# Output biases from rows weighted by GpSimd and summed by TensorE, in two attention layers

## The chip, the cores and the metric

The kernel runs on one core of a Trainium2 chip. Its time is that of the device in microseconds, the median of 3 runs. Beside it there is one execution taken by the hardware profiler, whose span runs from the first to the last instruction.

## The reference

Two layers in a row, each a group normalisation, a self-attention over 1024 positions of 256 channels, an output projection with a bias, and a residual. Batch 2, all in float32.

```python
xn = group_norm(x, gamma, beta)                      # 32 groups of 8 channels
q, k, v = xn @ wq + bq, xn @ wk + bk, xn @ wv + bv   # 1024 x 256 each
attn = softmax(q @ k.T / 16)                         # 1024 x 1024
out = (attn @ v) @ wp + bp + x
```

Because each row of `attn` sums to one, the bias of `v` contributes the same row `bv @ wp` to every output row. The kernel adds `bv @ wp + bp` once per output row. That vector of 256 numbers per layer is the output bias of the title.

## The kernel before

**Algebra.** The scores are computed as `xn @ A @ xn.T` with `A = wq @ wk.T`, and the values as `xn @ Wx` with `Wx = wv @ wp`, so that a unit (one image in one layer, four units in all) needs three kinds of large product: `t` (`A` times the normalised input), the scores `S`, and the values `V`, and then the attention product `O`. Each large product is made of three matmuls with rounded operands (`_hi` and `_lo` parts, whose sum is the float32 value): `L1081` to `L1083` for t, `L1108` to `L1110` for scores, `L1094` to `L1096` for values, `L1134` to `L1136` for attention.

**Order.** All engines run programs written out by hand, in the order of the code, with semaphores between them. There is no scheduler. PSUM holds seven banks used in a ring (`ring`) and one more, `X`. Bank 6 of the ring (`RING - 1`) serves the small things of the start: the warm-up products, group means and variances, and the output bias. Its later use by the third score tile waits for `dv_ob`, which says that the output bias was taken out.

**The start.** SyncE issues all loads in one queue: `wq`, `wk` of layer 0, image 0, `wv`, `wp`, then `wq`, `wk` of layer 1, `wide` of layer 0 (rows of the vectors copied to all 128 partitions), `wv`, `wp` of layer 1, `wide` of layer 1, then `moved` (image 1, in pieces of 128 bytes for the transposition by VectorE) and image 1 itself. Layers, units and images are counted from 0, as in the code. In the rows the numbers of buffers are left out, so `w_wp` is either layer's.

**TensorE's start** (in this order): transposes of the weights (`transpose_weight`, L939), of image 0 (L985), the product A of layer 0 (L948), one-column products of layer 0's `wp` with `bv` (L970), group means (L1021) and group variances (L1027), Wx of layer 0 (L957), the one-column products of layer 1, A of layer 1, the first half of Wx of layer 1, the first half of t, the second half of Wx, the second half of t, four transposes that spread the bias columns over all partitions (L978), and then the scores of the first half (chunk 0).

**The statistics.** VectorE sums up group statistics (`channel_statistics`, L637), TensorE averages over groups, VectorE adds epsilon (L653), GpSimd raises to the power -0.5 (`power`, L348), and VectorE makes gain and shift and normalises (L678). ScalarE rounds to `xn_hi` (L457), VectorE subtracts to `xn_lo` (L685). The t products read both.

**What follows on VectorE.** `t_lo` (L714), `A_lo` of layer 1, `out_bias` (L631), `Wx_lo` of layer 1 (L613), then image 1's transposes and statistics between the running maxima of chunk 0 (L732), the values' low parts (L721), and the query maxima and their shift (`neg_shift`, L746), which TensorE spreads over the partitions in `shift_to_all` (L1127). GpSimd adds the output bias to the image rows (`residual`, L359) and forms the low parts of the exponentials (`p_low`, L363).

## Time and profile before

| what | value |
|---|---|
| median of 3 runs | 253.14 us (253.07 to 253.24) |
| span of the profiled execution | 250.6 us |
| the profiled execution's own time beside its span | not given by the page |
| TensorE busy | 245.2 us, 98% of the span |
| VectorE busy | 187.2 us, 75% |
| ScalarE busy | 149.4 us, 60% |
| GpSimd busy | 125.1 us, 50% |
| mean granted TensorE clock | 0.999 |

The span is 2.5 us shorter than the median time, because it leaves out what lies before the first and behind the last instruction. A share of busy time is an average over the whole span, so it does not say which engine is waited for in a given stretch. The views used below are the chain of waits, which follows the work that ended last backwards from the last instruction, and timelines of single engines.

### The profile page before, as it was taken

How to read it: one execution, taken by the hardware profiler on the slowest of the kernel's cores; microseconds unless marked ns; L12 is line 12 of the kernel's file. 1: busy time of each engine (PE TensorE's matmuls, PEld its weight loads, DVE VectorE, ACT ScalarE, POOL GpSimd, SP SyncE). 2: the span in 40 equal slices, each digit the busy share in tenths (PEclk: the TensorE clock that was granted, in tenths of full speed). 3: DMA queues.
4: the chain of work that ended last, by engine and by line, in shares of the span. 5: the costliest groups of instructions: out<-in, count | busy, mean ns of one | idle time of the engine just before them, and what ended most of it. 6: DMA issues, size and time to landing. Idle time of an engine off the chain costs nothing.

```text
span 250.6 us, 4585 instructions
## 1 busy us (share of the span) xinstructions
PE 245.2 (98%) x1570; PEld 223.5 (89%) x1570; DVE 187.2 (75%) x490; ACT 149.4 (60%) x291; POOL 125.1 (50%) x151
## 2 busy tenths in 40 slices
PE   7999998999999999999999999999999999999995
PEld 6888888889998899889998899889998899889995
DVE  0688898888994798587975998587875798449804
ACT  3665543699994309831998508940998509740920
POOL 3010621485779306901797916901797918800870
PEclk9999999999999999999999999999999999999999
DMA  6999000000025002320142001320110000100112
GB/s 195 352 153 221 6 0 3 0 1 3 0 86 86 1 0 55 84 32 3 43 87 43 0 0 46 84 41 3 43 43 0 3 16 29 42 0 10 36 42 86
DMA packets 34767, 12.37 MB, mean 49 GB/s; under 512 B 26284, under 2 KB 34488, under 8 KB 34744
## 3 DMA queue, kind: packets, MB, share of 16 engines
q1 hardware_dynamic: 34720, 12.07, 20.0%
q8 instruction: 13, 0.21, 0.4%
q14 instruction: 10, 0.08, 0.1%
q10 hardware_dynamic: 24, 0.01, 0.0%
HBM read 7.88 MB, written 4.19 MB: 48 GB/s over the span
## 4 chain that ended last, share of the span: by engine, by line
PE 89%; DVE 6%; DMA 2%; issue 1%; ACT 1%; SPq 0%; DVEq 0%
PE ring L1134 12%; PE ring L1136 12%; PE ring L1135 12%; PE ring L1109 10%; PE ring L1110 10%; PE ring L1108 10%; PE ring L1081 3%; PE ring L1083 3%; PE ring L1082 3%; PE ring L1094 3%; PE ring L1096 3%; PE ring L1095 2%; DVE R L732 2%; DMA xnat<-in_x 2%; PE ring L948 1%; DVE xraw L593 1%
## 5 line engine op out<-in xcount | busy, mean ns | idle before, releaser
L363 POOL TENSOR_TENSOR P_lo<-S,P_hi 128x512 fp32r<-128x512 f32 x64 | 81.9, 1310 | 52.2 <-ACT S L503 52.1
L1134 PE MATMUL ring<-V,P_hi 128*128 128x258 f32 x256 | 72.7, 284 | 0.0
L1136 PE MATMUL ring<-V,P_lo 128*128 128x258 f32 x256 | 72.4, 283 | 0.0
L1135 PE MATMUL ring<-V,P_hi 128*128 128x256 f32 x256 | 72.3, 282 | 0.0
L502 ACT ACTIVATE P_hi<-S 128x512 fp32r<-128x512 f32 x64 | 40.4, 631 | 29.7 <-DVE S L791 29.7
L495 ACT COPY S<-ring 128x512 f32<-128x512 f32 x64 | 36.6, 590 | 31.4 <-PE ring L1110 30.3
L1108 PE MATMUL ring<-t_hi,xn_lo 128*128 128x512 f32 x128 | 49.9, 390 | 0.0
L1109 PE MATMUL ring<-t_lo,xn_hi 128*128 128x512 f32 x128 | 49.8, 389 | 0.0
L1110 PE MATMUL ring<-t_hi,xn_hi 128*128 128x512 f32 x128 | 49.8, 389 | 0.0
L1134 PEld LDWEIGHTS ring<-V,P_hi 128*128 128x128 f32 x256 | 48.5, 189 | 0.4
L1135 PEld LDWEIGHTS ring<-V,P_hi 128*128 128x128 f32 x256 | 48.4, 189 | 0.4
L1136 PEld LDWEIGHTS ring<-V,P_lo 128*128 128x128 f32 x256 | 48.5, 190 | 0.0
L732 DVE TENSOR_TENSOR R<-ring,R 128x512 f32<-128x512 f32 x48 | 32.9, 685 | 12.5 <-ACT S L495 10.9
L791 DVE TENSOR_TENSOR S<-X,S 128x512 f32<-128x512 f32 x64 | 41.1, 681 | 0.0
L503 ACT ACTIVATE S<-S 128x512 f32<-128x512 f32 x64 | 40.0, 625 | 0.0
L359 POOL TENSOR_TENSOR xnat<-xnat,out_bias 128x256 f32<-128x256 f32 x32 | 22.5, 746 | 13.4 <-DVE out_bias L631 13.4
L1110 PEld LDWEIGHTS ring<-t_hi,xn_hi 128*128 128x128 f32 x128 | 24.0, 188 | 5.0
L1108 PEld LDWEIGHTS ring<-t_hi,xn_lo 128*128 128x128 f32 x128 | 24.0, 188 | 4.7
L1109 PEld LDWEIGHTS ring<-t_lo,xn_hi 128*128 128x128 f32 x128 | 24.0, 188 | 4.7
L348 POOL TENSOR_TENSOR r<-var_e,minus_half 128x2 f32<-128x2 f32 x4 | 2.8, 709 | 37.3 <-DVE var_e L653 37.3
L721 DVE TENSOR_TENSOR V<-ring,V 128x256 fp32r<-128x256 f32 x32 | 13.4, 418 | 8.9 <-ACT V L488 8.9
L1094 PE MATMUL ring<-Wx_hi,xn_lo 128*128 128x258 f32 x64 | 18.6, 290 | 0.0
(117 smaller groups left out, 356.3 us busy)
## 6 DMA issues: line engine op xcount, KB each, us to landing
xnat<-in_x SPq DMA_DIRECT2D x8, 256.0 KB, 4.6
between<-xnat SPq DMA_DIRECT2D x16, 128.0 KB, 1.8
out<-xnat SPq DMA_DIRECT2D x16, 128.0 KB, 1.7
moved<-in_x SPq DMA_DIRECT2D x8, 128.0 KB, 4.7
moved<-between SPq DMA_DIRECT2D x16, 64.0 KB, 2.4
moved<-between SPq DMA_DIRECT2D x32, 32.0 KB, 2.0
w_wq<-in_L_conv_wq SPq DMA_DIRECT2D x2, 256.0 KB, 4.3
w_wk<-in_L_conv_wk SPq DMA_DIRECT2D x2, 256.0 KB, 4.5
```

Source lines behind the costliest of these rows:

```text
L363: nc.gpsimd.tensor_tensor(P_lo[:, exp_of(c, kb), :], S[:, tile_of(c, kb), :], P_hi[:, exp_of(c, kb), :].bitcast(F32), ALU.subtract).then_i ...
L495: nc.scalar.copy(S[:, tile_of(c, kb), :], bank_of("S", c, kb)[:]).then_inc(ac_S, 1)
L502: nc.scalar.activation(P_hi[:, exp_of(c, kb), :], S[:, tile, :], ACT.Exp)
L503: nc.scalar.activation(S[:, tile, :], S[:, tile, :], ACT.Exp).then_inc(ac_P, 1)
L732: nc.vector.tensor_tensor(R[:], bank_of("S", c, kb)[:], earlier, ALU.max).then_inc(dv_R, 1)
L791: nc.vector.tensor_tensor(tile, X[:], tile, ALU.add).then_inc(dv_D, 1)
L1108: nc.tensor.matmul(bank[:], xn_lo[:, kc, keys], t_hi[:, kc, cols], start=(kc == 0), stop=False)
L1109: nc.tensor.matmul(bank[:], xn_hi[:, kc, keys], t_lo[:, kc, cols], start=False, stop=False)
L1110: last = nc.tensor.matmul(bank[:], xn_hi[:, kc, keys], t_hi[:, kc, cols], start=False, stop=(kc == KC - 1))
L1134: nc.tensor.matmul(bank[:, 0:C + 2], P_hi[:, tile, mine], v[:, kb, 0:C + 2], start=(kb == 0), stop=False)
L1135: nc.tensor.matmul(bank[:, 0:C], P_hi[:, tile, mine], v[:, kb, C + 2:VX], start=False, stop=False)
L1136: last = nc.tensor.matmul(bank[:, 0:C + 2], P_lo[:, tile, mine], v[:, kb, 0:C + 2], start=False, stop=(kb == NB - 1))
```

## The change

The output bias of a layer is `bv @ wp + bp`. Before, TensorE multiplied blocks of `wp` with the column `bv` (8 products of one column in all), VectorE added `bp` as a column (`bias_columns`), TensorE transposed the broadcast columns so that every partition held the row, and VectorE copied the result out of PSUM. After, GpSimd multiplies the rows of `wp` by `bv` per partition, adds the two blocks and splits the sum into a rounded and a remaining part (`weighted_rows`). TensorE multiplies both parts with a 128x128 matrix of ones, which sums over the partitions and leaves the row in each of them. VectorE adds `bp`, which now comes with `wide`, as it takes the result out of PSUM. The second half of layer 1's Wx product moves from the middle of the t products to behind the first half.

```diff
-WIDE = VECTORS[3:5]
+WIDE = VECTORS[3:6]
...
-        bias_col = sb("bias_col", [P, LAYERS, KC])
+        ones = sb("ones", [P, P], F32R)
...
+            weighted = sb("weighted", [P, LAYERS, KC, C], stack=early)
+            weighted_hi = sb("weighted_hi", [P, LAYERS, C], F32R, stack=early)
+            weighted_lo = sb("weighted_lo", [P, LAYERS, C], F32R, stack=early)
...
+            def weighted_rows(l):
+
+                r = l * NV + VECTORS.index("bv")
+                pool.wait_ge(ld_w[l, "wp"], 16)
+                for k in range(KC):
+                    nc.gpsimd.tensor_scalar(weighted[:, l, k, :], w_raw[l, "wp"][:, k, :], vec_cols[:, k, r:r + 1],
+                                            None, ALU.mult).then_inc(po_bv, 1)
+                pool.wait_ge(po_bv, 5 * l + 2)
+                nc.gpsimd.tensor_tensor(weighted[:, l, 0, :], weighted[:, l, 0, :], weighted[:, l, 1, :], ALU.add
+                                        ).then_inc(po_bv, 1)
+                pool.wait_ge(po_bv, 5 * l + 3)
+                nc.gpsimd.tensor_copy(weighted_hi[:, l, :], weighted[:, l, 0, :]).then_inc(po_bv, 1)
+                pool.wait_ge(po_bv, 5 * l + 4)
+                nc.gpsimd.tensor_tensor(weighted_lo[:, l, :], weighted[:, l, 0, :], weighted_hi[:, l, :].bitcast(F32),
+                                        ALU.subtract).then_inc(po_bv, 1)
...
+            weighted_rows(0)
             power(0)
+            weighted_rows(1)
             pool.wait_ge(dv_ob, 1)
...
+            nc.vector.memset(ones[:].bitcast(F32), 1.0)
...
-            def bias_columns():
-                dve.wait_ge(pe_ob, LAYERS)
-                for l in range(LAYERS):
-                    nc.vector.tensor_tensor(bias_col[:, l, :], bias_bank(l), vec_cols[:, :, l * NV + VECTORS.index("bp")],
-                                            ALU.add).then_inc(dv_oc, 1)
-
             def output_biases():
                 dve.wait_ge(pe_oa, 1)
-                nc.vector.tensor_copy(out_bias[:, :, :], ring[RING - 1][:, :].rearrange("p (l c) -> p l c", l=LAYERS)
-                                      ).then_inc(dv_ob, 1)
+                for l in range(LAYERS):
+                    dve.wait_ge(ld_wide[l], 16)
+                    last = nc.vector.tensor_tensor(out_bias[:, l, :], ring[RING - 1][:, l * C:(l + 1) * C],
+                                                   wide[:, l, WIDE.index("bp"), :], ALU.add)
+                last.then_inc(dv_ob, 1)
...
-            def output_bias(l):
-
-                pe.wait_ge(ld_w[l, "wp"], 16)
-                if l:
-
-                    pe.wait_ge(dv_stat, VARE)
-                r = l * NV + VECTORS.index("bv")
-                for k in range(KC):
-                    for kd in range(KC):
-                        last = nc.tensor.matmul(bias_bank(l)[:, k:k + 1], w_raw[l, "wp"][:, kd, k * P:(k + 1) * P],
-                                                vec_cols[:, kd, r:r + 1], start=(kd == 0), stop=(kd == KC - 1))
-                last.then_inc(pe_ob, 1)
-
             def output_biases_to_all():
-                pe.wait_ge(dv_oc, LAYERS)
-                for l in range(LAYERS):
-                    for k in range(KC):
-                        last = nc.tensor.transpose(ring[RING - 1][:, l * C + k * P:l * C + (k + 1) * P],
-                                                   bias_col[:, l, k:k + 1].to_broadcast([P, P]), ident[:])
-                last.then_inc(pe_oa, 1)
+
+                pe.wait_ge(po_bv, 5 * LAYERS)
+                nc.tensor.matmul(ring[RING - 1][:], ones[:], weighted_hi[:, :, :].rearrange("p l c -> p (l c)"),
+                                 start=True, stop=False)
+                nc.tensor.matmul(ring[RING - 1][:], ones[:], weighted_lo[:, :, :].rearrange("p l c -> p (l c)"),
+                                 start=False, stop=True).then_inc(pe_oa, 1)
...
-            output_bias(0)
             mean_of_groups(0)
...
-            output_bias(1)
             for mc in range(KC):
                 A_product(1, mc)
-            Wx_product(1, 0)
+            for mc in range(KC):
+                Wx_product(1, mc)
...
-            Wx_product(1, 1)
```

On TensorE, from layer 0's transposed `wv` to the first t product, the program before reads:

```order
L939 MATMUL X<-ident,w_wv 128x128 x4
L970 MATMUL ring<-vec_cols,w_wp 128x1 x4
L1021 MATMUL ring<-mv,group_mean 128x2
L939 MATMUL ring<-ident,w_wq 128x128 x4
L939 MATMUL ring<-ident,w_wk 128x128 x4
L1027 MATMUL ring<-var_c,group_mean 128x2
L957 MATMUL ring<-w_wp,wvT 128x256 x4
L939 MATMUL X<-ident,w_wv 128x128 x4
L970 MATMUL ring<-vec_cols,w_wp 128x1 x4
L948 MATMUL ring<-wkT_bk,wqT 128x257 x4
L957 MATMUL X<-w_wp,wvT 128x256 x2
L1081 MATMUL ring<-xn_hi,A_lo 128x512
```

and of the changed program the same place reads as follows (its lines are those of the changed file: L953 transposes weights, L962 is A, L971 is Wx):

```order
L953 MATMUL X<-ident,w_wv 128x128 x4
L1022 MATMUL ring<-mv,group_mean 128x2
L953 MATMUL ring<-ident,w_wq 128x128 x4
L953 MATMUL ring<-ident,w_wk 128x128 x4
L1028 MATMUL ring<-var_c,group_mean 128x2
L971 MATMUL ring<-w_wp,wvT 128x256 x4
L953 MATMUL X<-ident,w_wv 128x128 x4
L962 MATMUL ring<-wkT_bk,wqT 128x257 x4
L971 MATMUL X<-w_wp,wvT 128x256 x4
L1081 MATMUL ring<-xn_hi,A_lo 128x512
```

Both groups of four one-column products are gone, and the Wx product of layer 1 is there in full (x4 where x2 stood) ahead of t.

On GpSimd, from the copies of `bk` into the weights to layer 0's first residual, the program before has three rows:

```order
L393 COPY wkT_bk<-vec_cols 128x2 x2
L348 TENSOR_TENSOR r<-var_e,minus_half 128x2
L359 TENSOR_TENSOR xnat<-xnat,out_bias 128x256 x8
```

and the changed one has:

```order
L408 COPY wkT_bk<-vec_cols 128x2 x2
L354 TENSOR_SCALAR weighted<-w_wp,vec_cols 128x256 x2
L357 TENSOR_TENSOR weighted<-weighted 128x256
L360 CAST weighted_hi<-weighted 128x256
L362 TENSOR_TENSOR weighted_lo<-weighted,weighted_hi 128x256
L347 TENSOR_TENSOR r<-var_e,minus_half 128x2
L354 TENSOR_SCALAR weighted<-w_wp,vec_cols 128x256 x2
L357 TENSOR_TENSOR weighted<-weighted 128x256
L360 CAST weighted_hi<-weighted 128x256
L362 TENSOR_TENSOR weighted_lo<-weighted,weighted_hi 128x256
```

Five rows of layer 0 now stand ahead of the power (L348, now L347), five of layer 1 behind it.

## Rows read from the trace of the kernel before

**Rows 1.** The page, part 1: busy time, share of the span, instructions.
```profile
PE 245.2 (98%) x1570; PEld 223.5 (89%) x1570; DVE 187.2 (75%) x490; ACT 149.4 (60%) x291; POOL 125.1 (50%) x151
```

**Rows 2.** TensorE's waits: who waited for whom, us in total, times, longest.
```profile
...
PE X L1127 <- DVE neg_shift L746: 0.7, 1, 0.7
...
```

**Rows 3.** The chain of waits, 8 to 43 us: start, us, what.
```profile
...
10.51 0.79 PE ring L970 x8
11.30 0.23 PE ring L1021 x2
...
14.90 0.79 PE ring L970 x8
...
17.53 0.86 PE X L957 x4
...
21.20 0.86 PE X L957 x4
...
24.63 0.25 PE ring L1083
24.91 0.70 ACT t_hi L481
...
26.38 0.60 DVE out_bias L631
26.98 0.66 DVE Wx_lo L613 x2
...
42.09 0.65 PE X L1127 x4
...
```

**Rows 4.** Timeline of VectorE: start us, us, instruction, count.
```profile
10.65 0.39 DVE L637 BATCH_NORM_AGGREGATE mv<-bn 128x2 f32<-128x24 f32 x2
...
16.16 1.28 DVE L685 TENSOR_TENSOR xn_lo<-xraw,xn_hi 128x512 fp32r<-128x512 f32 x2
...
19.43 1.28 DVE L685 TENSOR_TENSOR xn_lo<-xraw,xn_hi 128x512 fp32r<-128x512 f32 x2
```

**Rows 5.** Timeline of TensorE's products: first and middle of t, the four transposes.
```profile
18.04 0.58 PE L1081 MATMUL ring<-xn_hi,A_lo 128*128 128x512 f32 x1
...
21.71 0.58 PE L1081 MATMUL ring<-xn_hi,A_lo 128*128 128x512 f32 x1
...
24.70 0.60 PE L978 MATMUL ring<-ident,bias_col 128*128 128x128 f32 x4
...
25.06 0.48 PE L1108 MATMUL ring<-t_hi,xn_lo 128*128 128x512 f32 x1
```

**Rows 6.** DMA: layer 0's `wp`, `moved`; each with its landing times.
```profile
4.34 0.47 SPq L282 DMA_DIRECT2D w_wp<-in_L_conv_wp  x1
...
DMA to landing us min/median/max: 5.5/6.2/6.8
...
L305 SPq DMA_DIRECT2D moved<-in_x x8: 432/875/3763, 8.3 to 18.6; - x8
...
DMA to landing us min/median/max: 4.0/4.7/8.0
```

**Rows 7.** GpSimd: timeline rows, and the summary of L363 (ns min/median/max).
```profile
12.97 0.72 POOL L348 TENSOR_TENSOR r<-var_e,minus_half 128x2 f32<-128x2 f32 x1 [7.41 <-DVE var_e L653]
27.05 5.63 POOL L359 TENSOR_TENSOR xnat<-xnat,out_bias 128x256 f32<-128x256 f32 x8 [13.36 <-DVE out_bias L631]
...
63.34 1.70 POOL L363 TENSOR_TENSOR P_lo<-S,P_hi 128x512 fp32r<-128x512 f32 x1 [2.96 <-ACT S L503]
...
L363 POOL TENSOR_TENSOR P_lo<-S,P_hi x64: 1280/1302/1695, 48.8 to 241.5; 128x512 fp32r<-128x512 f32 x64
```

**Rows 8.** Stretches: length, busy us by engine, granted clock, DMA share, GB/s.
```profile
3.70:5.80 2.10, 1.69 (x12) 1.24 (x11) 0.18 (x1) 0.96 (x2) 0.31 (x2) 1.00 0.91 264
5.80:9.00 3.20, 2.86 (x20) 2.44 (x21) 1.29 (x4) 1.96 (x5) 0.00 (x0) 1.00 1.03 351
```

**Rows 9.** VectorE's L685, all eight (ns min/median/max).
```profile
L685 DVE TENSOR_TENSOR xn_lo<-xraw,xn_hi x8: 678/682/684, 16.2 to 65.6; 128x512 fp32r<-128x512 f32 x8
```

More of the change, by code:

```diff
@@ L188, in two_attention_layers @@
         po_bk = sem("po_bk")
+        po_bv = sem("po_bv")
         po_resid = sem("po_resid")
@@ L198, in two_attention_layers @@
         pe_Wx = sem("pe_Wx")
-        pe_ob = sem("pe_ob")
         pe_oa = sem("pe_oa")
@@ L226, in two_attention_layers @@
         dv_Wx = sem("dv_Wx")
-        dv_oc = sem("dv_oc")
         dv_ob = sem("dv_ob")
@@ L244, in two_attention_layers @@
         dv_O = sem("dv_O")
-        def bias_bank(l):
-            return ring[RING - 1][:, (l + 1) * KC:(l + 2) * KC]
         def mean_bank(v):
@@ L705, in _ @@
             normalise(0, range(2, 4))
-            bias_columns()
             Wx_low(0, 1)
```

## The prediction

> **What bounds the kernel now.** I read the page's engine shares first: TensorE is busy for 98% of the span [rows 1]. So the question is where TensorE still stands still, and whether an edit touches that place or TensorE's own queue. The list of TensorE's waits has one entry behind the ninth microsecond: 0.7 us in which the transposes of `shift_to_all` (L1127) wait for VectorE's `neg_shift` [rows 2]. Behind it TensorE runs to the tail without a wait that the list shows, so what moves that point moves the end.
>
> The chain of waits shows what leads up to it [rows 3]. From 8.6 to 24.9 us it is TensorE in its own order: weights, the two groups of one-column products (L970), the products A and Wx, the t products. At 24.91 it passes over `t_hi` on ScalarE to `t_lo`, `out_bias` and `Wx_lo` on VectorE, stays on VectorE for image 1's statistics and the running maxima, and comes back to TensorE at 42.09. So there are two stretches to price: TensorE before 24.9 us, and VectorE from 25.6 to 42.0 us. Between them TensorE is not the bound: it has 0.7 us to spare at 42.09.
>
> **The change part by part.**
>
> *The one-column products.* Two groups of 8 (4 products, each shown as two passes) take 0.79 us each in the chain [rows 3]. The second group, at 14.90, stands between transposes and `A_product(1, 0)`, which wait for nothing there: removing it gives 0.79. The first, at 10.51, stands ahead of the group means (L1021), which need the aggregate that VectorE finishes at 10.65 + 0.39 = 11.04 [rows 4]; the means begin at 11.30. So at most 0.26 is to be had. A part goes to the handover and to the empty array: four transposes behind the wait at 42.09 take 0.65 [rows 3], four in a full queue 25.06 - 24.70 = 0.36 [rows 5]. That difference, 0.29, would eat all of it. The bounds are 0 and 0.2; I take 0.05, near the lower one, as the row after a wait is the same situation.
>
> A rule would price the group otherwise. The row gives 0.79 / 8 = 0.10 us per one-column pass. The Trainium skill's page "TensorE: Matmul & The Clock Gate", section "Wait — 56ns, not 53.3ns?", says that starts of small matmuls lie no closer than about 25 ns: by that alone a group would be worth 0.2 us and the sum would shrink to a gain of about 0.2. The trace disagrees with that as a price for these products; the same page's section on LDWEIGHTS (columns / 1.2 GHz, 107 ns for 128) comes near the row, so it is the weights that are paid for.
>
> *Wx of layer 1* (the second of two, as the code counts). Its second half (L957, 0.86 us at 21.20) moves ahead of the t products, behind the first half at 17.53 [rows 3]. The start of the t products goes 0.86 later, their end doesn't move. So t starts at 18.04 - 0.79 - 0.05 + 0.86 = 18.06, as before; its second half, which began at 21.71 [rows 5], begins 0.84 earlier, at 20.87, and its last product, which ended at 24.63 + 0.25 = 24.88, ends 0.84 earlier too. Are the operands there? `xn_lo` for the first half is done from 16.16 + 0.64 = 16.80 on, for the second from 19.43 + 0.64 = 20.07 on [rows 4]. The tighter slack is 20.87 - 20.07 = 0.80. The two small additions `bias_col` that leave VectorE between them can only widen it.
>
> *GpSimd's rows.* Per layer two products by a scalar, an addition, a rounding and a subtraction, each 128x256. Layer 0's five stand ahead of `power(0)`, on which the normalisation, `xn_lo` and the t products hang. They start when `wp` of layer 0 has landed: 4.34 + 5.5 = 9.84 [rows 6]. `power(0)` started at 12.97 [rows 7] and may slip by the slack of 0.80, to 13.77: the five may take 3.9 us. The nearest rows: 8 two-input additions of this shape take 5.63, 0.70 each; the P_lo subtraction that also writes rounded output takes 1.30 for twice the elements, 0.65 [rows 7]. As an upper bound all five at 0.70, with 0.06 for each of four handovers (an estimate, twice the 0.03 us between the last t product's end and `t_hi`): 3.75. As a lower one, the three with one input at half: 2.6. I take 3.2, so they end near 13.0, delay `power(0)` by nothing or 0.1, and cost nothing. If that cover is gone, each further microsecond comes out as one of delay. Layer 1's five follow `power(0)` and are needed only by the product at 24 us; with GpSimd idle until 27.05 [rows 7] they are hidden.
>
> [...]
>
> *The sum with ones.* Four transposes (0.36) give way to two products of 512 columns. A 512-column product in the stream takes 0.25 in the chain [rows 3], so 0.5: TensorE loses some 0.14, behind the last t product. The 0.7 us of its wait at 42.09 cover it.
>
> *VectorE.* `out_bias` was one copy of 512 columns, 0.60 in the chain; it becomes two additions of 256 out of PSUM. Two such subtractions (`Wx_lo`) take 0.66 [rows 3]: +0.06 on the path. Bounds: 0, and 0.23 if a start of their own adds half of one such addition, 0.17. `bias_col` was off the path here; the memset of `ones` falls in the idle first microseconds.
>
> *DMA.* `wide` grows from 2 to 3 KB in each of 128 partitions, 256 to 384 KB, twice. At the 351 GB/s of the early stretch [rows 8] that is 0.37 us for what is queued behind the first and 0.75 behind both. `moved` is behind both; the last of its eight issues starts at 18.6, and its first reader on VectorE starts behind `Wx_lo`, at 26.98 + 0.66 = 27.64 (26.86 after) [rows 3, 6]. With the median of 4.7 us to landing it is there at 23.3, and with 0.75 more still in time.
>
> *Sum*: -0.79 - 0.05 + 0.06 = -0.78 us on the path to `neg_shift`, and from there TensorE carries it to the end. The profiled execution has a span of 250.6 us, the timed runs a median of 253.14; the 2.5 us between lie around the span and don't change. 253.14 - 0.78 = 252.36. With the bounds: 252.1 (-0.79 - 0.2) to 252.6 (-0.79 + 0.23).
>
> **The rivals.**
> 1. *Partly absorbed, within 0.2%.* The gain must pass VectorE's chain of 16 us, where score copies, `moved` and the running maxima each have a few tenths to spare. For it: `moved` took up to 8.0 us to land at worst [rows 6]; were that the last issue (from about 18.6), it would land at 26.6 + 0.75 = 27.35 against 26.86, 0.49 late. Or the five rows take 4.3 instead of 3.2 and `power(0)` is 0.4 too late. Against it: of the eight issues one alone took 3763 ns where the median took 875, and the longest landing is more likely that one's than the last one's. Time: 253.14 - 0.78 + 0.45 = 252.8. Chance 0.20.
> 2. *GpSimd becomes the gate: slower.* One mechanism, the five rows ahead of `power(0)`. Nothing in the trace shows a 128x256 product by a per-partition scalar on GpSimd. If the two cost 1.6 each (more than twice the addition), the five take 5.5, end at 15.3, and t starts 1.6 late: 253.14 - 0.78 + 1.6 = 253.9. It decides from 3.9 + 0.78 = 4.7 us on. Against it: the two-input addition of this size takes 0.70, and here there is one input. Chance 0.06.
> 3. *The port.* GpSimd and VectorE disturb each other while both run. The row: P_lo at 63.34 took 1.70 against a median of 1.30 while VectorE ran two `xn_lo` subtractions, but these took 678 to 684 ns in all eight cases, GpSimd idle or not [rows 7, 9]. So GpSimd pays 0.2 per such neighbour and VectorE nothing; layer 0's rows meet only statistics and 2-column operations, layer 1's meet `xn_lo` and have time. If VectorE paid the same 0.4 for two `xn_lo` operations that the slack doesn't hold, twice: 253.14 - 0.78 + 0.8 = 253.2. Chance 0.03. The Trainium skill's "GPSIMD Engine Reference", section 8 ("Key points"), states the contention without a price or a loser.
> 4. *The clock.* TensorE will stand idle for about 0.6 us before the group means. It was idle for 0.4 of 2.1 us at 3.7 to 5.8 at a granted clock of 1.00, 2.4 GHz [rows 8]. A fall to 1.2 GHz that doubles 1 us of work costs 1 us: 253.4. Chance 0.02.
> 5. *The products were cheap.* The chain gives a busy stretch to whoever is in it; if only a quarter of the 0.79 is the passes' own and the rest is the start of what follows, the removal returns 0.2: 253.14 - 0.2 - 0.05 + 0.06 = 252.95. Against it: the half of Wx behind A and the half between the t products take the same 0.86 [rows 3], whatever stands ahead. Chance 0.03. The Trainium skill's rule on the spacing of small matmuls ("TensorE: Matmul & The Clock Gate", section "Wait — 56ns, not 53.3ns?") would have it so.
>
> **How the numbers follow.** The forecast has 0.66. A measurement of this kernel can tell some 0.2%, 0.5 us, from no change. Faster by more: the forecast and a little of rival 1, 0.69. Within: most of rival 1, and rivals 3 to 5 for the most part, 0.24. Slower: rival 2 and half of rival 4, 0.07. In the order of rivals: 0.66, then 0.20, 0.06, 0.03, 0.02, 0.03. The range from 252.0 to 253.0 holds the forecast with its bounds, rival 1 and rival 5, and leaves out rivals 2 to 4, 0.11; alone the forecast would span 252.1 to 252.6.
>
> **What would show it.** In the new trace: the group means 0 to 0.2 earlier; L1127's wait ending near 41.3; `t_hi` last starting near 24.1; `power(0)` starting by 13.1, at most 13.8; the two `out_bias` additions 0.66 together; TensorE's wait before L1127 0.5 to 0.7. Wrong it is if the t products wait for `xn_lo` (GpSimd's rows too long), or if TensorE's 42.09 stays while 24.91 moves (something on VectorE's stretch waits).

## The result: slower by 0.45%, where 0.3% faster was forecast

| | before | after |
|---|---|---|
| median | 253.08 us (253.01 to 253.24, 6 runs) | 254.05 us (253.74 to 255.48, 6 runs) |
| ratio to before, 95% interval | | 1.0045 (1.0031 to 1.0059) |
| profiled execution: own time, span | span 250.6 | 254.13, span 252.4 |

The forecast was 252.36 us, its range 252.0 to 253.0; the measured time lies outside. Two different things cost the time. I read them in the order in which they stand in the span: the stretch to the transposes of `shift_to_all` (L1127), and what is behind it.

**The page.** First part, busy time of each engine, and the instructions:

```profile
span 252.4 us, 4559 instructions
...
PE 245.4 (97%) x1552; PEld 222.0 (88%) x1552; DVE 188.6 (75%) x490; ACT 149.1 (59%) x291; POOL 133.2 (53%) x161
```

A pass is one matmul row of the trace; each of the 8 one-column products shows as two passes, a transpose and a product with rounded operands as one. TensorE has 18 passes fewer than in [rows 1] (16 of one column and 4 transposes gone, 2 products of 512 new) and nearly the same busy time (245.4 us for 245.2); VectorE has the same 490 instructions and is busy 1.4 us longer.

**The waits.** The list by engine and line: us in total, times, longest:

```profile
PE ring L1022 <- DVE mv L652: 0.9, 2, 0.7
...
PE ring L1081 <- DVE xn_lo L700: 0.8, 2, 0.5
...
PE X L1127 <- DVE neg_shift L760: 0.6, 1, 0.6
DVE xraw L611 <- DMA moved<-between: 0.6, 1, 0.6
```

The second is the sign that the prediction had named for "GpSimd's rows too long": both halves of t wait for `xn_lo`. The last has no counterpart before at all.

**GpSimd's timeline**, 8 to 30 us (start, us, engine, line, operation, tiles, count, idle before):

```profile
10.71 1.84 POOL L354 TENSOR_SCALAR weighted<-w_wp,vec_cols 128x256 f32<-128x256 f32 x2 [4.74 <-DMA w_wp<-in_L_conv_wp]
12.63 0.73 POOL L357 TENSOR_TENSOR weighted<-weighted 128x256 f32<-128x256 f32 x1
13.44 0.40 POOL L360 CAST weighted_hi<-weighted 128x256 fp32r<-128x256 f32 x1
13.91 0.73 POOL L362 TENSOR_TENSOR weighted_lo<-weighted,weighted_hi 128x256 fp32r<-128x256 f32 x1
14.60 0.73 POOL L347 TENSOR_TENSOR r<-var_e,minus_half 128x2 f32<-128x2 f32 x1
15.31 1.84 POOL L354 TENSOR_SCALAR weighted<-w_wp,vec_cols 128x256 f32<-128x256 f32 x2
17.23 0.78 POOL L357 TENSOR_TENSOR weighted<-weighted 128x256 f32<-128x256 f32 x1
...
18.63 1.18 POOL L362 TENSOR_TENSOR weighted_lo<-weighted,weighted_hi 128x256 fp32r<-128x256 f32 x1
```

Layer 0's five occupy GpSimd from 10.71 to 14.64, 3.93 us. The product by a per-partition scalar takes 0.92, more than the addition of two tiles (0.73); of the three operations with one input only the rounding (0.40) is as cheap as I had made all three.

**VectorE's timeline**, 11 to 21 us:

```profile
11.12 0.39 DVE L652 BATCH_NORM_AGGREGATE mv<-bn 128x2 f32<-128x24 f32 x2
...
13.14 0.22 DVE L668 TENSOR_SCALAR var_e<-ring,eps 128x2 f32<-128x2 f32 x1
...
15.36 0.16 DVE L675 TENSOR_TENSOR r0sq<-r 128x2 f32<-128x2 f32 x1 [1.61 <-POOL r L347]
...
16.75 1.54 DVE L693 TENSOR_SCALAR xraw<-xraw,gain,shift 128x512 f32<-128x512 f32 x2
...
18.55 1.81 DVE L700 TENSOR_TENSOR xn_lo<-xraw,xn_hi 128x512 fp32r<-128x512 f32 x2
...
20.98 0.99 DVE L693 TENSOR_SCALAR xraw<-xraw,gain,shift 128x512 f32<-128x512 f32 x2
...
22.23 1.28 DVE L700 TENSOR_TENSOR xn_lo<-xraw,xn_hi 128x512 fp32r<-128x512 f32 x2
```

The same operations in the kernel before:

```profile
13.72 0.16 DVE L660 TENSOR_TENSOR r0sq<-r 128x2 f32<-128x2 f32 x1 [0.45 <-POOL r L348]
...
14.90 1.00 DVE L678 TENSOR_SCALAR xraw<-xraw,gain,shift 128x512 f32<-128x512 f32 x2
```

`var_e` is done at 13.36, the power starts at 14.60. And the pairs at 16.75 and 18.55, which run while layer 1's five rows are on GpSimd, take 1.54 and 1.81; the same pairs behind them take 0.99 and 1.28, as in the kernel before (1.00 above, 1.28 in [rows 4]). From the start of `r0sq` to the end of the first `xn_lo` pair it is 5.00 us where it was 3.72. Of the `xn_lo` pair itself only the second operation is slow. The query for that tile, 18 to 21 us (ns min/median/max):

```profile
L700 DVE TENSOR_TENSOR xn_lo<-xraw,xn_hi x2: 675/944/1214, 18.6 to 19.2; 128x512 fp32r<-128x512 f32 x2
```

The one that began at 18.55, ahead of GpSimd's subtraction at 18.63, took its usual 0.68; the one that began at 19.15, inside that subtraction, took 1.21.

**The chain of waits**, 4 to 44 us:

```profile
4.76 5.85 DMA w_wp<-in_L_conv_wp
...
10.71 1.85 POOL weighted L354 x2
...
14.64 0.69 POOL r L347
...
23.05 0.47 PE ring L1081
...
26.10 0.70 ACT t_hi L498
...
27.49 0.75 DVE out_bias L645 x2
...
43.35 0.65 PE X L1127 x4
```

It begins with the landing of `wp` (4.76 + 5.85 = 10.61, where I had 9.84), goes over GpSimd's rows, the power and VectorE, and only then enters TensorE. L1127 starts at 43.35, 1.26 us later than in [rows 3]. Behind it the last matmul comes 205.86 us later, where it was 205.32 before: 0.54 more, at the wait for `moved<-between`.

**A yardstick.** The start is not the same in every execution of one kernel: the aggregate of image 0 (`BATCH_NORM_AGGREGATE` on VectorE) starts at 10.65 in the profile of before, and at 11.33 and 13.15 in two more profiles of the same kernel (below). So I compare two distances: A, from that aggregate to the transposes of `shift_to_all`, and B, from there to the start of the last matmul. Before: A 31.44, B 205.32. After: A 32.23, B 205.86. Together +1.33; the medians say +0.97. The rest would lie in the start, which the profiles don't settle: the aggregate of the changed kernel is at 11.12, later than in one profile of before and earlier than in two.

### The profile page after: what moved, and what is told of

It is laid out like the page before. It is cut to its first block, busy times and chain, and to the rows that moved or that the text cites. A ratio compares the mean times of both kernels' runs of the same rounds, so it can differ in the third digit from the quotient of the medians.

```text
span 252.4 us, 4559 instructions
## 1 busy us (share of the span) xinstructions
PE 245.4 (97%) x1552; PEld 222.0 (88%) x1552; DVE 188.6 (75%) x490; ACT 149.1 (59%) x291; POOL 133.2 (53%) x161
## 4 chain that ended last, share of the span: by engine, by line
PE 60%; DVE 20%; DMA 5%; SPq 4%; issue 4%; ACT 3%; POOL 2%; DVEq 0%; ACTq 0%
PE ring L1134 9%; PE ring L1136 9%; PE ring L1135 9%; PE ring L1108 7%; PE ring L1109 7%; PE ring L1110 7%; DVE R L746 3%; DVE S L805 3%; SPq L304 3%; DMA w_wp<-in_L_conv_wp 2%; DMA between<-xnat 2%; PE ring L1081 2%; DVE xraw L611 2%; PE ring L1082 2%; PE ring L1083 2%
## 5 line engine op out<-in xcount | busy, mean ns | idle before, releaser
L347 POOL TENSOR_TENSOR r<-var_e,minus_half 128x2 f32<-128x2 f32 x4 | 2.9, 714 | 30.4 <-DVE var_e L668 30.4
```

## The experiments

The first four experiments ask what GpSimd's rows cost, and in which way: the power comes late (theory 1), or VectorE is slower beside GpSimd (theory 2).

### e1_no_rows, e2_rows0_only, e3_rows1_only, e4_power_first

```diff
+            no_rows(0)
+            no_rows(1)
             pool.wait_ge(dv_const, 1)
...
-            weighted_rows(0)
             power(0)
-            weighted_rows(1)
```

This is e1: `no_rows` is two memsets of zero for a layer, in the idle start. e2 keeps `weighted_rows(0)`, with memsets for layer 1 behind the power; e3 keeps `weighted_rows(1)`, with memsets for layer 0 at the start. Memsets in place of rows leave bv @ wp out of the output of that layer. e4 is complete: `power(0)` stands ahead of both `weighted_rows`.

> The changed kernel without GpSimd's weighted rows: both parts are set to zero in the idle start, so the output lacks bv @ wp in both layers. Everything else, TensorE's order, the sum with ones, the wider load and VectorE's two additions, stays. Theory (only the rows on GpSimd were mis-priced; TensorE's and VectorE's terms of the prediction hold): the power starts as soon as its variance is there, within 0.1 us, t waits for nothing, and the time is 0.6 to 0.9 us under before, 252.2 to 252.5. Rival (the removal of the column products returns little, or the wider load delays the start by the 0.4 us seen in the changed kernel's profile): 252.8 or more.

> The changed kernel with layer 0's rows alone; layer 1's are set to zero behind the power, so layer 1's output lacks bv @ wp. Theory, two causes that add up: the rows ahead of the power delay it by some 1.2 us (they take 3.9 us from the landing of wp on), and the rows behind it slow VectorE's normalisation and xn_lo by some 1.3 us through the shared access to SBUF; t can hide 0.8 of the sum. So this run shows the first cause alone: power delayed by about 1.2, VectorE's first normalisation back at 0.54 us each, and a time about 0.4 us over the run without rows, near 252.7. Rival, the delay ahead of the power is all there is: the time is that of the changed kernel, 254.0.

> The changed kernel with layer 1's rows alone, behind the power; layer 0's are set to zero in the idle start, so layer 0's output lacks bv @ wp. Theory of the two causes: the power is on time, but VectorE between r0sq and the second xn_lo takes 4.9 us instead of 3.6, as in the changed kernel, and with 0.8 of slack the time is about 0.5 us over the run without rows, near 252.8. Rival, the delay ahead of the power is all there is: VectorE's stretch takes 3.6 us again and the time is that of the run without rows.

> All of the change, but the power stands ahead of both layers' rows, which then run one after the other, some 7.9 us, beside VectorE's normalisation and both pairs of xn_lo. Rival theory, only the delay of the power costs: 252.3 to 252.5, all of the predicted gain. Theory of the two causes: the power is on time, but VectorE loses 1.3 us before the first half of t and up to 1.0 more before the second; less 0.8 of slack that is 1 to 1.5 us over the run without rows, 253.3 to 253.9, so little is won against the changed kernel's 254.05.

| | median (runs), beside before 252.96 (31 runs) | ratio, 95% | A | B |
|---|---|---|---|---|
| e1, no rows | 253.15 (12) | 1.0002 (0.9986 to 1.0018) | 30.57 | 206.25 |
| e2, layer 0's | 253.27 (12) | 1.0016 (0.9994 to 1.0039) | 30.58 | 206.09 |
| e3, layer 1's | 253.48 (12) | 1.0020 (1.0003 to 1.0037) | 30.89 | 206.58 |
| e4, power first | 254.42 (8) | 1.0062 (1.0031 to 1.0093) | 31.83 | 206.21 |

e1's A is 0.87 below that of before, a little more than the forecast's whole sum, and 1.66 below that of the changed kernel: that is what the rows cost. e4 takes the power's delay away (`r0sq` starts 3.06 behind the aggregate, as the 3.07 of before) and is still slow. VectorE's timeline of e4 shows by what way:

```profile
14.36 0.16 DVE L675 TENSOR_TENSOR r0sq<-r 128x2 f32<-128x2 f32 x1 [0.43 <-POOL r L347]
...
15.78 1.55 DVE L693 TENSOR_SCALAR xraw<-xraw,gain,shift 128x512 f32<-128x512 f32 x2
...
17.59 1.81 DVE L700 TENSOR_TENSOR xn_lo<-xraw,xn_hi 128x512 fp32r<-128x512 f32 x2
```

So both theories hold, each with a part. e3, with layer 1's rows alone, lies between: its `xn_lo` pair takes 1.68, from `r0sq` to its end it is 4.29 where 4.9 was expected, and its A is 0.32 above e1's. e2 could not price the delay: the execution that was profiled started late (aggregate at 13.59), while `wp` landed at 10.74, and the five rows were done at 14.74, before the power was wanted (15.82). Its VectorE runs at its old pace (1.00 and 1.28), which fits theory 2, since layer 0's rows stand beside nothing large.

But e1 was expected to give back the forecast's gain and doesn't. Its B is 0.93 above that of before. All four have a wait for `moved<-between` of 0.7 to 1.3 us, near 170 us. So there is a second cause.

### b1_before, b2_before, e5_shifted, e6_no_columns

Is the late wait a matter of the execution, of where tiles lie, or of TensorE's program? b1 and b2 are the kernel before, unchanged. e5 is the kernel before with 480 unused bytes per partition, meant to put the tiles behind them where the changed kernel has them; the tiles of the start that lie behind the wider `wide` are not moved with it. e6 is the kernel before without the 16 one-column passes (`bias_col` is then bp alone, so bv @ wp is left out):

```diff
-            output_bias(0)
...
-            output_bias(1)
```

> The kernel before, unchanged, for a second profile. In all five profiles of changed kernels the aggregate of the group statistics came 0.4 us or more later than in the one profile of before, the first four transposes took 1.07 us where they took 0.76, and VectorE later waited 0.6 to 1.3 us for image 1's pieces of layer 1. Theory (that one execution was a fortunate one, and the start varies from run to run whatever the kernel): here the aggregate comes at 11.0 to 11.4 too, and the late wait is there. Rival (something in the change makes the start slower): all three are as in the first profile.

> The same once more, a third profile of the kernel before, with the same two readings.

> The kernel before with one unused tensor of 480 bytes per partition put in behind the bias columns, so that everything behind it lies where it lies in the changed kernel. Theory (the place in SBUF is nothing): no change in time and the same profile as before. Rival (the place is what slows the start): 0.3 to 0.7 us slower, first transposes 1.07 us, wait for the pieces of layer 1.

> The kernel before without the 16 one-column passes of TensorE: the bias columns hold bp alone, so the output lacks bv @ wp. Nothing else is changed: transposes, copy, load and the place of Wx stay. It prices the one term of the prediction that carries it. Theory (0.79 + 0.05 off TensorE's path, all of it passed on): 0.7 to 0.9 us faster than before. Rival (the start or VectorE's stretch swallows it, as the changed kernel without rows, which came out the same as before within 0.16%, suggests): within 0.3 us of before.

| | median (runs), beside before 253.09 (23 runs) | ratio, 95% | aggregate | A | B | late wait |
|---|---|---|---|---|---|---|
| b1 | 254.88 (1) | | 13.15 | 31.43 | 205.29 | none |
| b2 | 253.06 (1) | | 11.33 | 31.44 | 205.28 | none |
| e5 | 253.14 (12) | 0.9999 (0.9976 to 1.0021) | 10.77 | 31.39 | 205.38 | none |
| e6 | 252.43 (12) | 0.9972 (0.9955 to 0.9989) | 11.02 | 30.53 | 206.18 | 1.0 |

The places of the tiles moved by e5 do nothing. The late wait comes when passes are taken from TensorE, with or without GpSimd's rows. e6's A is 30.53 and e1's 30.57, so moving `Wx`, the two products with ones and the second addition of `output_biases` together cost 0.04.

The DMA view says where. Stretches of 3 us in 40 slices; `between<-xnat` is one of two writes that follow each other by 3.05 us, and on queue 8 one transfer of 0.02 MB appears (the slice with 218 GB/s when it stands alone). Before, 150 to 153 us:

```profile
GB/s 0 0 0 0 0 0 0 0 0 0 0 0 0 0 0 0 14 218 369 328 369 287 151 14 0 0 0 0 0 0 218 0 0 0 0 0 0 0 0 0
...
q8 instruction: 1, 0.02, 1.8%
...
between<-xnat SPq DMA_DIRECT2D x1, 128.0 KB, 1.7
```

The changed kernel, 155 to 158 us:

```profile
GB/s 0 0 0 0 0 0 0 0 0 382 273 355 328 300 192 28 0 0 0 0 0 0 0 0 0 14 14 0 14 14 0 14 14 14 14 0 0 0 0 0
...
q8 instruction: 1, 0.02, 2.6%
...
between<-xnat SPq DMA_DIRECT2D x1, 128.0 KB, 3.3
```

Before, the transfer of queue 8 stands 1.0 us behind the start of the first write, in the gap ahead of the second. In the changed kernel it begins in the same slice as the second write, and that write ends with a thin tail of 14 GB/s over 0.75 us that begins 0.7 us behind the burst: it lands after 3.3 us instead of 1.7. SyncE waits for it before it issues the eight reads `moved<-between` of 32 KB, and the chain of the changed kernel then goes through `154.85 3.27 DMA between<-xnat` to unit 3's statistics and the group means.

### e7_second_group_out, e8_padded, e9_after_padded, e10_rows_by_tensor

Queue 8 is marked "instruction". If it brings TensorE's program at fixed places of it, fewer passes ahead of that place let it come later against the work (theory F); the rival is that any earlier TensorE meets the writes worse (theory G). e7 removes one group alone:

```diff
-            output_bias(1)
```

e8 and e9 fill TensorE's program up again with products of one column that nothing reads. e8 is e7 with 6 of them in the warm-up in place of 2 of its 6 products of 128 columns; e9 is the changed kernel with this edit:

```diff
-            keep_running(6)
+            keep_running(3)
+            one_column(8)
...
+            one_column(4)
             mean_of_groups(0)
```

e10 is a complete kernel of a third kind: the row of bv @ wp comes ready and in all partitions out of TensorE, with bv's column broadcast as the stationary operand; bp is added from wide rows as in the changed kernel. It also has filler in the warm-up, 10 one-column products in place of 4 of the 6 of 128 columns.

```diff
-                        last = nc.tensor.matmul(bias_bank(l)[:, k:k + 1], w_raw[l, "wp"][:, kd, k * P:(k + 1) * P],
-                                                vec_cols[:, kd, r:r + 1], start=(kd == 0), stop=(kd == KC - 1))
+                    last = nc.tensor.matmul(ring[RING - 1][:, l * C:(l + 1) * C],
+                                            vec_cols[:, kd, r:r + 1].to_broadcast([P, P]),
+                                            w_raw[l, "wp"][:, kd, :], start=(kd == 0), stop=(kd == KC - 1))
```

> The kernel before without the second group of one-column products (16 passes become 8); the first group stays, its result is not read, the bias columns hold bp alone, so the output lacks bv @ wp. Open is where the late wait of unit 3's statistics comes from (VectorE waits 0.6 to 1.3 us for moved<-between near 167 us in the six kernels whose TensorE has 16 passes fewer, in none of the four that have them). Theory F: TensorE's own instructions are fetched by DMA (13 transfers on queue 8), at fixed places of its program; with 16 passes fewer the fetch that began 0.95 us behind the start of the first of two writes to `between` begins 2.9 us behind it, together with the second write, which then takes 3.3 us instead of 1.8. With 8 fewer it should begin about 1.9 behind, between the two: no late wait, shift_to_all 30.65 us behind the aggregate (31.44 before, less 0.79), 252.3 us. Theory G: any earlier TensorE meets the writes worse, and the place in the program is nothing: a late wait of 0.6 to 1.3 here too, and 252.6.

> The kernel before without both groups' use: the first group stays as an unread filler in its own place, the second is gone from the path, and the warm-up at the start holds 8 one-column passes more than before (4 products of 128 columns and 6 of one column, where there were 6 of 128), so TensorE's program has as many passes as before; the output lacks bv @ wp. Theory F: the fetch stands 0.95 us behind the first write's start as before, no late wait, shift_to_all 30.65 us behind the aggregate, 252.3 us as in the kernel with 8 fewer. Theory G: late wait 0.6 to 1.3, 252.6 or more. If one-column passes at the start let the granted clock fall, or end later than 4.05 us, it is slower by what the start then shows.

> The changed kernel with 18 one-column passes of no use: 8 in TensorE's wait ahead of the group means, the others in the warm-up at the start (3 products of 128 columns and 8 of one, for 6 of 128), so that everything behind stands at the place in TensorE's program that it had before the change. Theory F: the fetch is back between the two writes, the late wait of 0.6 us on VectorE is gone, and the time falls from 254.05 by 0.5 to 0.6 (last matmul minus shift_to_all 205.3 instead of 205.86): 253.5. Theory G: 254.05 and the wait stays. The rows of GpSimd and VectorE's slower operations beside them stay in either case: shift_to_all 32.2 us behind the aggregate.

> A complete version meant to beat both: no work on GpSimd. TensorE multiplies bv's column, broadcast as the stationary operand, with wp (two products of 256 columns per layer, 1.03 us for four passes of 257 in A's rows); layer 0 in the wait of 0.7 us ahead of the group means, layer 1 in place of the four transposes behind t; bp is added out of wide rows as in the changed kernel, Wx stays in its old order, and 12 one-column passes pad the start. Expected from the rows: -0.79 -0.05 for the groups, +0.33 for layer 0's 1.03 in a wait of 0.7, +0.06 for the two additions, +0 to 0.1 for layer 1's 1.03 in place of 0.36 against 0.66 of slack: -0.45 to -0.35, 252.7. Theory F: no late wait. Theory G: with it 253.2. If the wait ahead of the means is only the 0.26 of the profiled execution before, 0.4 more.

| | median (runs), beside before 253.06 (17 runs) | ratio, 95% | aggregate | A | B | late wait |
|---|---|---|---|---|---|---|
| e7 | 252.19 (12) | 0.9981 (0.9956 to 1.0006) | 13.01 | 30.54 | 205.25 | none |
| e8 | 254.48 (6) | 1.0063 (1.0045 to 1.0081) | 13.41 | 30.54 | 205.30 | none |
| e9 | 255.64 (4) | 1.0105 (1.0092 to 1.0119) | 14.35 | 31.06 | 205.40 | none |
| e10 | 255.67 (4) | 1.0107 (1.0092 to 1.0121) | 15.08 | 30.74 | 205.37 | none |

The times of e8 to e10 miss what I expected of them (252.3, 253.5 and 252.7): in the start, where most of the filler stands, a one-column pass takes 0.21 us (e8: 12 of them in 2.42 us), and the aggregate starts 2 to 4 us later than in b2. B doesn't depend on that, and it speaks for F: in all four it is back at 205.3 to 205.4 and the wait is gone. G is out, since e7's TensorE is 0.9 us earlier and meets no late wait. The count of passes says the same. From the span's start to the start of queue 8's transfer, before and in the changed kernel (in the order of the columns: length, then PE, PEld, DVE, ACT, POOL, each with its instructions, granted clock, DMA share, GB/s):

```profile
0.00:152.25 152.25, 149.74 (x927) 134.98 (x928) 120.58 (x329) 92.76 (x184) 71.70 (x98) 1.00 0.26 61
```

```profile
0.00:155.68 155.68, 151.80 (x927) 135.50 (x928) 123.40 (x332) 94.53 (x188) 81.65 (x110) 1.00 0.24 61
```

In both, TensorE has begun 927 passes by then. The changed kernel has 18 fewer in its start, so its 927th stands later in the work. In all sixteen traces of this case it is 925 to 931.

e7's median (252.19, expected 252.3) has executions with early and late starts in it, from 251.44 to 254.70, so its interval is wide. Its trace tells what each group is worth. One group out gives 31.44 - 30.54 = 0.90, both give 0.91: the second group is worth 0.90 and the first 0.01.

e9 gives the price of the two ways of GpSimd as well, by the accident of its late start: `wp` had landed, the rows began at 9.83 and the power waited for `var_e`, not for them. Between e1 and e9 it is 31.06 - 30.57 = 0.49, VectorE's slowing alone behind the slack; from the changed kernel to e9 it is 32.23 - 31.06 = 1.17, as much as the power's delay (`r0sq` 4.24 us behind the aggregate there, 3.07 in e9). One trace each stands behind this split.

### e11_rows_by_tensor_unpadded, e12_after_gap_filled

e11 is e10 without the filler. e12 is the changed kernel with 8 one-column passes in TensorE's wait ahead of the group means and nothing else:

```diff
+            one_column(4)
             mean_of_groups(0)
```

> The complete version with bv's column as the stationary operand, without the filler in the start, where a one-column pass took 0.21 us and made the whole run start 2 to 3 us late. TensorE has 12 passes fewer than the kernel before, so by theory F the fetch begins about 2.4 us behind the first write's start, just ahead of the second at 2.9: no late wait, shift_to_all 30.74 us behind the aggregate as with the filler (31.44 before), 252.4 us. Rival: 12 fewer is already too many, the fetch meets the second write, a late wait of 0.6 to 1.3 and 252.9 to 253.2.

> The changed kernel with 8 one-column passes of no use in TensorE's wait of 0.9 us ahead of the group means (0.12 us each there), nothing changed in the start; 10 passes fewer than before instead of 18. Theory F: the fetch stands about 2.2 us behind the first write's start, between the writes: no late wait, the last matmul 205.3 us behind shift_to_all instead of 205.86, 253.5 us against 254.05. Theory G (an earlier or later phase of the writes, not the place in the program): wait and time stay, 254.05. shift_to_all 32.2 us behind the aggregate as in the changed kernel; in the version whose start was late by the filler it was 31.06, because wp had landed by then: if the landing of wp decides, a late start here too gives less than 32.2.

| | median (runs), beside before 253.10 (18 runs) | ratio, 95% | A | B | late wait |
|---|---|---|---|---|---|
| e11 | 252.50 (252.00 to 252.71, 8) | 0.9973 (0.9963 to 0.9983) | 30.75 | 205.39 | none |
| e12 | 253.42 (253.06 to 254.58, 11) | 1.0020 (1.0008 to 1.0032) | 32.08 | 205.40 | none |

Both came out within 0.1 us of what F gave (252.4 and 253.5). e12 has more work than the changed kernel and its ratio is 0.0025 lower, 0.6 us, with intervals that touch only at their ends (1.0008 to 1.0032, and 1.0031 to 1.0059). Of the 0.6, 0.46 is in B (205.40 for 205.86) and 0.15 in A. Its DMA view, 155 to 158 us:

```profile
GB/s 218 0 0 0 0 0 0 0 0 0 0 0 68 205 369 341 341 260 110 14 14 27 0 0 0 0 0 0 0 0 0 0 0 0 0 0 0 0 0 0
...
q8 instruction: 1, 0.02, 2.0%
...
between<-xnat SPq DMA_DIRECT2D x1, 128.0 KB, 2.0
```

The transfer of queue 8 is ahead of the second write by 0.9 us, and the tail is short. Over the kernels, the place of that transfer behind the start of the first write, the passes that TensorE has fewer than before, and the landing of the second write:

| passes fewer | 0 (before, b1, b2, e5, e9) | 8 (e7) | 10 (e12) | 12 (e11) | 16 (e6) | 18 (after; e1 to e4) |
|---|---|---|---|---|---|---|
| behind the first write's start, us | 1.0 | 1.8 | 2.1 | 2.3 | 2.9 | 3.1; 3.0 to 3.2 |
| landing of the second write, us | 1.7 | 2.0 | 2.0 | 2.4 | 3.5 | 3.3; 3.3 to 3.8 |

That is 0.115 us for each pass, about what a one-column pass in the stream takes (0.12). The second write starts at 3.05, and its landing grows as the transfer comes near it. e8 and e10 have as many passes as before but stand at 1.5 and 0.7, with 931 and 925 passes begun; their semaphore waits differ too, and whether that is the reason isn't shown.

e11 is the version that beats both: 252.50 against 253.10 and 254.05. In TensorE's timeline its layer 1 stands where the transposes stood:

```profile
11.04 1.03 PE L960 MATMUL ring<-w_wp,vec_cols 128*128 128x256 f32 x4
...
24.47 1.03 PE L960 MATMUL ring<-w_wp,vec_cols 128*128 128x256 f32 x4
...
42.08 0.65 PE L1110 MATMUL X<-ident,neg_shift 128*128 128x128 f32 x4 [0.39 <-DVE neg_shift L736]
```

The wait at `shift_to_all` is down from 0.66 in the kernel before to 0.39, not gone: TensorE's slack had room for it.

## Why the prediction was wrong, step by step

**The one-column products: right, and better than forecast.** The second group was put at 0.79 and is worth 0.90 (e7). The first was put at 0.05 and is worth 0.01 (e7 against e6). The rival that they were cheap is out: one-column passes take 0.12 us in the stream of e12's timeline (8 in 0.95). With it goes the spacing rule of the Trainium skill's "TensorE: Matmul & The Clock Gate" ("Wait — 56ns, not 53.3ns?") as a price for them, which would be about 0.025 us a pass.

**`Wx` moved, the sum with ones, `out_bias` in two: right.** Together 0.04 (e1 against e6), forecast 0.06.

**GpSimd's rows: the step that failed.** It read that the five "take 3.2, so they end near 13.0, delay `power(0)` by nothing or 0.1, and cost nothing". They take 3.93 and start at 10.71, and the power is 1.17 us late (`r0sq` 4.24 us behind the aggregate, 3.07 before). Two terms were off. The size: "the three with one input at half" holds for the rounding alone; the product by a scalar had no row, and it costs more than the dearest row of its shape. The upper bound of 3.75 was built from that dearest row and was no bound. The start: 9.84 came from the landing of a single issue in a single profile, of an execution whose start was early; it was 10.61 in the next, and 9.74 to 11.29 over the sixteen. Measured from the aggregate, the rows began 0.4 us later than I had them and took 0.7 longer, which together is nearly all of the delay.

**The port: dismissed on a row that didn't bear on it.** This is the second half of the failed step. Rival 3 had a chance of 0.03, because in [rows 9] VectorE's `xn_lo` took the same with GpSimd idle or busy. But of those eight only the one that began at 63.19 lay beside `P_lo` (63.34) for more than 0.04 us, and it began ahead of it; so the row had no case of an `xn_lo` that begins while GpSimd works. Beside layer 1's rows VectorE pays: 1.54 for 1.00, 1.81 for 1.28, and some of the 2-column operations 0.25 for 0.16, in the changed kernel, in e4, e9 and e12 alike. That is 5.00 - 3.72 = 1.28 us to the end of the first `xn_lo` pair. Over all sixteen traces, the seven `xn_lo` operations that begin 0.3 to 0.7 us ahead of the end of one of GpSimd's took 0.88 to 1.22 and ended 0.55 us behind that end, as if they had waited for it; the others took 0.67 to 0.69; `Wx_lo`, which reads PSUM, is not slowed there (0.41 at 18.22 in the changed kernel). The Trainium skill's "GPSIMD Engine Reference", section 8 ("Key points"), which I had put beside this rival, was the better guide than my row: it names VectorE operations with two SBUF inputs, and `xn_lo` is one (1.21 for 0.68).

**The slack was right and was spent once.** I had 0.80 of it for the t products and held it against the power's delay alone. The two costs share it: 1.17 + 1.28 - 0.80 = 1.65, and the measured cost of the rows is 32.23 - 30.57 = 1.66. Each of these terms comes from one trace, so that they meet within 0.01 is in part luck. With the products' 0.91 back and 0.04 for the rest, A changes by +0.79, as the traces have it. Rival 2 had the power's delay alone with the whole slack taken off, rival 3 VectorE's alone, at 0.8 with the slack already spent; no case had both.

**What no step had: the second write.** "From there TensorE carries it to the end" was wrong by 0.54 us. Behind L1127 TensorE's work hangs on a DMA chain in unit 2 (two writes, eight reads, two more writes, eight reads), which has about 1 us to spare: the second write landed 1.6 us late and 0.54 of it came through. What moved the collision is the length of TensorE's program (18 passes). Filler in the changed kernel took the late wait away and brought B back by 0.46 (e12).

**The frame.** I took 253.14 - 250.6 = 2.5 us as time around the span. It is 1.7 to 1.9 in the later runs, e7's apart (up to 2.4); the profiled execution was one whose start was 0.7 us earlier than that of b2, whose time is the median's. The sum didn't hang on that, but the landing of `wp` and the 0.26 us ahead of the means did.

Left open: e6's trace has the late wait and B 206.18, and yet its median is 0.66 us under before, where A + B change by -0.05. Its transfer stands 0.2 us ahead of the second write, so a small shift may save an execution from it; I have one trace of e6 and can't tell. Why one part of the write lags behind the transfer isn't shown either, only that it does, and by how much.

## What to carry to other kernels

An operation that moves to an idle engine is priced by a row of that very operation and shape; where there is none, the dearest row of another operation is no upper bound, and the slack that is to cover it may be spent only once over all that draws on it. GpSimd's work of this kind beside VectorE's critical stretch was paid by VectorE here, so before an idle GpSimd is taken for free, look at which VectorE operations would begin while it works, and whether anything waits for them. And after any change in the number of instructions, look for a wait far behind the edit: here removing 18 passes moved an instruction transfer onto a write 140 us later, and if taking work out doesn't pay, count the passes and look at queue 8 before giving up the edit.

## What the runs showed of the hardware that was not expected

- GpSimd: 128x256 by a per-partition scalar 0.92 us, addition 0.73, rounding 0.40. Beside VectorE's normalise and `xn_lo` they take 0.92, 0.78 and 0.47, and the subtraction 1.18 for 0.73, all in the changed kernel's trace.
- VectorE beside them, single operations in the changed kernel: 128x512 normalise 0.68 and 0.94 for 0.54, subtraction 0.68 and 1.21 for 0.68. A subtraction that begins ahead of GpSimd's operation keeps its time, and one that begins inside it is the slow one; `Wx_lo`, which reads PSUM, keeps its 0.41.
- An instruction transfer of 0.02 MB that starts together with a 128 KB write lengthens its landing from 1.7 to 3.3 us (after), with a tail of 14 GB/s, and to as much as 3.8 (e3).
- The instruction transfer of queue 8 between 152 and 157 us starts when TensorE has begun 925 to 931 passes, in each of sixteen traces of programs with 1552 to 1570.
- TensorE comes to its full pace at different times in the start, though the granted clock of b1 reads 1.00, the level of 2.4 GHz, in each microsecond from the first to the twelfth. The rows of two profiles of one kernel (b1, and b2 below it) show the same four passes of 257 columns in 1.92 and in 1.14 us:

```profile
7.52 1.92 PE L948 MATMUL ring<-wkT_bk,wqT 128*128 128x257 f32 x4
```

```profile
6.92 1.14 PE L948 MATMUL ring<-wkT_bk,wqT 128*128 128x257 f32 x4
```

In the profile of before they take 1.03. The three aggregates are at 13.15, 11.33 and 10.65, while A and B agree within 0.04 us: what these three executions of one kernel differ by lies ahead of the aggregate. A filler of one-column passes there made it late in three kernels of three (13.41 to 15.08); why isn't shown.
